# Packed means of one graph layer go to two tables, one for each half tile, and the node stage adds both

## What is computed

```python
h = jnp.maximum(_layernorm(x, axis=-1), 0.0)
msg = jnp.concatenate([h[src], edge_attr_128], axis=-1) @ W1 + b1
msg_sum = jax.ops.segment_sum(msg, dst, num_segments=N)
deg = jax.ops.segment_sum(jnp.ones((E,)), dst, num_segments=N)
node_msg = msg_sum / jnp.maximum(deg, 1.0)[:, None]
out = node_msg + (node_msg @ W2 + b2)
x = x + jnp.where(out >= 0, out, SLOPE * out)
```

## Time and profile before

| | before |
|---|---|
| median of three runs | 6092.15 us (6090.74 to 6095.57) |
| the profiled execution | 6094.43 us, of which the span is 6092.7 us |
| granted TensorE clock, mean | 0.813 |
| busy in the span | PE 62%, DVE 64%, POOL 49%, ACT 33% |
| stage e0 | first gather at 153 us, last store issued at 982 us |
| stage n0 | first load at 987 us, last scatter ends at 1534 us |

### The profile page before, as it was taken

One profiled execution on the slowest core, in us unless ns is written; L12 is line 12 of the kernel. 1 busy time (PEld: TensorE's weight loads), 2 busy tenths in 40 slices (PEclk: granted clock), 3 DMA queues, 4 the chain that ended last, 5 costly groups with the idle time before them and its releaser, 6 DMA issues. The chain is left out here.

```text
span 6092.7 us, 90449 instructions
## 1 busy us (share of the span) xinstructions
PE 3790.4 (62%) x17060; PEld 2576.8 (42%) x17060; DVE 3911.8 (64%) x12523; ACT 2020.2 (33%) x4450; POOL 2987.2 (49%) x2764
## 2 busy tenths in 40 slices
PE   0788884333079997669976557666600098888840
PEld 0466663333047776554445545555500043433310
DVE  8555555888058885334455546665568788888856
ACT  0444452333012222125556642222234433333310
POOL 0644442777177640000037767777710167777730
PEclk9888885555589999999986768988855599999975
DMA  6566665776955542774467767777678611111149
GB/s 224 148 158 159 159 158 155 232 220 201 352 146 136 143 116 59 235 242 155 152 201 234 229 197 143 132 131 130 108 226 272 196 34 38 43 46 48 48 151 377
DMA packets 983330, 994.95 MB, mean 163 GB/s; under 512 B 207537, under 2 KB 645313, under 8 KB 983059
## 3 DMA queue, kind: packets, MB, share of 16 engines
q1 hardware_dynamic: 673795, 628.11, 35.3%
q0 software_dynamic: 131904, 146.31, 12.5%
q10 hardware_dynamic: 177488, 218.95, 10.2%
HBM read 560.95 MB, written 466.16 MB: 169 GB/s over the span
## 5 line engine op out<-in xcount | busy, mean ns | idle before, releaser
L703 POOL DMA_INDIRECT at_first_table<-n_h,n_first_edge x784 | 791.2, 1009 | 1247.9 <-ACT n_h L271 890.6
L2467 PE MATMUL e_m<-e_by_rel,rel_w 128*128 128x512 f32 x1568 | 708.3, 606 | 0.0
L695 POOL DMA_INDIRECT e_xs<-x_table,e_idx x392 | 377.2, 962 | 515.4 <-POOLq L2357 396.2
L695 POOL DMA_INDIRECT e_x<-x,e_idx x392 | 375.1, 957 | 451.4 <-ACT e_h L271 232.8
L695 POOL DMA_INDIRECT e_hs<-h_table,e_idx x392 | 422.3, 1077 | 278.7 <-PE e_hs L1528 155.5
L2381 DVE SCALAR_TENSOR_TENSOR e_by_rel<-e_y,e_part_t 128x512 f32<-128x512 f32 x784 | 476.4, 679 | 28.1 <-PE e_y L2482 20.0
L703 POOL DMA_INDIRECT rel_sum_table<-e_res,e_again x392 | 393.8, 1005 | 148.9 <-issue 124.9
L2467 PEld LDWEIGHTS e_m<-e_by_rel,rel_w 128*128 128x128 f32 x1568 | 298.2, 195 | 340.3 <-issue 340.3
L2459 PE MATMUL e_t<-ident,e_part 128*128 128x128 f32 x392 | 67.1, 298 | 572.4 <-ACT e_part L271 440.0
L1008 PE MATMUL n_m<-n_mean,n_pick 128*128 128x129 f32 x784 | 203.4, 440 | 338.8 <-DVE n_pick L1073 315.2
L711 POOL DMA_INDIRECT sum_table<-e_res,e_target x196 | 309.7, 1580 | 133.2 <-issue 55.4
(11 more groups left out here) (372 smaller groups left out, 10391.2 us busy)
## 6 DMA issues: line engine op xcount, KB each, us to landing
x_table<-n_x ACTq DMA_DIRECT2D x294, 256.0 KB
n_x<-x_table SPq DMA_DIRECT2D x294, 256.0 KB
e_hd<-at_first_table SPq DMA_DIRECT2D x196, 256.0 KB
mean_runs_table<-e_packed SPq DMA_DIRECT2D x196, 130.0 KB
n_mean<-mean_runs_table SPq DMA_DIRECT2D x392, 65.0 KB
at_first_table<-prep_zero ACTq DMA_DIRECT2D x1, 25088.0 KB
e_edge<-edge128T SPq DMA_DIRECT2D x98, 256.0 KB
e_keep<-col_tab_table SPq DMA_DIRECT2D x196, 128.0 KB
```

Source lines behind the costliest of these rows:

```text
L695: pool.indirect_dma_start(out=tile[:, t, :], out_offset=None, in_=table, in_offset=bass.IndirectOffsetOnAxis(ap=idx[:, col + t:col + t + 1 ...
L703: pool.indirect_dma_start(out=table, out_offset=bass.IndirectOffsetOnAxis(ap=idx[:, t:t + 1], axis=0), in_=tile[:, t, :], in_offset=None, ...
L2467: ins = pe.matmul(flat(at(ps_m, u - 6)), k.rel_w[:, r, :], at(by_rel, u - 6)[:, r, :], start=(r == 0), stop=(r == RELS - 1))
```

## The change

`mean_runs` becomes two tables, `mean_runs[0]` for the halves 0 and `mean_runs[1]` for the halves 1. `e_packed` holds for each half four blocks, two with rows and two of zeros, and each store writes all four (512 rows of 520 bytes): since the other half's rows are now missing in a table, zeros must reach over their place. Each table has a chain of its own: `placed[h]` counts its landings, and a store waits only for the one before it in its own table. The stores keep their places in SP's body, each with a `sem_inc` more. ACT waits for the same two stores of step i - 15, now by two semaphores. At the start DVE zeroes the blocks behind the rows in all four buffers, and SP stores zeros over the first 256 rows of table 1. In n0 each of the four loads fetches 128 rows of both tables; the difference of destination and block is made for both (`near`), `k.local` is the greater of the two, `n_pick` is twice as wide, and PE adds the two by two matmuls into one sum, eight for each step.

```diff
@@ mean_edges
-        packed, packed_ready = ph.made("packed", [P, TILES, RUN_COLS], 4)
-        placed = ph.sem("placed")
+        packed, packed_ready = ph.made("packed", [P, HALVES, TILES, RUN_COLS], 4)
+        placed, packed_zero = [ph.sem(f"placed{h}") for h in range(HALVES)], ph.sem("packed_zero")
+        sp_turn = ph.sem("sp_turn")
@@ SP
-                if not (isinstance(j, int) and j == 0 and h == 0):
-                    sp.wait_ge(placed, (j * HALVES + h) * 16)
-                sp.dma_start(run_rows(scratch["mean_runs"], begins[2 * h], HALVES),
-                             at(packed, u)[:, HALVES * h:HALVES * h + HALVES, :]).then_inc(placed, 16)
+                if h or not (isinstance(j, int) and j == 0):
+                    sp.wait_ge(placed[h], (j + h) * 16)
+                sp.sem_inc(sp_turn, 1)
+                sp.dma_start(run_rows(scratch["mean_runs"][h], begins[2 * h], TILES), at(packed, u)[:, h, :, :]
+                             ).then_inc(placed[h], 16)
@@
                     sp.wait_ge(packed_ready, w + 1)
+                    sp.sem_inc(sp_turn, 1)
                     place_half(w, u, begins, 0)
@@
+            sp.wait_ge(packed_zero, 1)
+            sp.dma_start(scratch["mean_runs"][1, 0:HALVES * P, :].rearrange("(b p) d -> p b d", p=P),
+                         packed[0][:, 1, HALVES:TILES, :]).then_inc(placed[1], 16)
             run_steps(sp, body, S, 16, 20)
-            sp.wait_ge(placed, HALVES * 16 * S)
+            for h in range(HALVES):
+                sp.wait_ge(placed[h], 16 * (S + h))
@@ DVE
+            for slot in packed:
+                ins = dve.memset(slot[:, :, HALVES:TILES, :], 0.0)
+            ins.then_inc(packed_zero, 1)
@@ ACT
                     if begun(j - 4):
-                        act.wait_ge(placed, (j - 3) * HALVES * 16)
+                        for b in range(HALVES):
+                            act.wait_ge(placed[b], (j - 3 + b) * 16)
                     for b in range(HALVES):
-                        ins = act.activation(at(packed, u - 11)[:, HALVES * b:HALVES * b + HALVES, :], ps_c[b][:, :, :],
-                                             ACT.Copy)
+                        ins = act.activation(at(packed, u - 11)[:, b, 0:HALVES, :], ps_c[b][:, :, :], ACT.Copy)
@@ mean_nodes
-        mean, mean_in = ph.loaded("mean", [P, TILES, RUN_COLS])
-        local_ready = ph.sem("local_ready")
-        pick, pick_ready = ph.made("pick", [P, TILES, P])
+        mean, mean_in = ph.loaded("mean", [P, TILES, HALVES, RUN_COLS])
+        near, near_ready = ph.made("near", [P, TILES, HALVES])
+        pick, pick_ready = ph.made("pick", [P, TILES, HALVES, P])
@@ SP
-                        sp.dma_start(at(mean, u)[:, t, :], scratch["mean_runs"][bass.ds(begins[t], P), :]
+                        sp.dma_start(at(mean, u)[:, t, :, :],
+                                     scratch["mean_runs"][:, bass.ds(begins[t], P), :].rearrange("h p c -> p h c")
                                      ).then_inc(at(mean_in, u), 16)
@@ PE
-                        ins = pe.matmul(at(ps_m, u - 1)[t // HALVES][:, t % HALVES, :], at(pick, u - 1)[:, t, :],
-                                        at(mean, u - 1)[:, t, 0:D + 1], start=True, stop=True)
+                        for h in range(HALVES):
+                            ins = pe.matmul(at(ps_m, u - 1)[t // HALVES][:, t % HALVES, :], at(pick, u - 1)[:, t, h, :],
+                                            at(mean, u - 1)[:, t, h, 0:D + 1], start=(h == 0), stop=(h == HALVES - 1))
@@ DVE
-                    local = k.local[:, bass.ds(i, 1), :].rearrange("p a t -> p (a t)")
-                    dve.tensor_tensor(local, at(mean, u)[:, :, D + 1],
-                                      k.block_at[:, bass.ds(i, 1), :].rearrange("p a t -> p (a t)"), ALU.subtract
-                                      ).then_inc(local_ready, 1)
-                    dve.wait_ge(local_ready, i + 1)
+                    dve.tensor_tensor(at(near, u)[:, :, :], at(mean, u)[:, :, :, D + 1],
+                                      k.block_at[:, bass.ds(i, 1), :].rearrange("p a t -> p (a t)").unsqueeze(2)
+                                      .broadcast_to([P, TILES, HALVES]), ALU.subtract).then_inc(near_ready, 1)
+                    dve.wait_ge(near_ready, i + 1)
+                    dve.tensor_tensor(k.local[:, bass.ds(i, 1), :].rearrange("p a t -> p (a t)"), at(near, u)[:, :, 0],
+                                      at(near, u)[:, :, 1], ALU.max)
                     if begun(i - 2):
                         dve.wait_ge(mean_done, i - 1)
-                    dve.tensor_tensor(at(pick, u)[:, :, :],
-                                      k.place_row[:, 0:P].unsqueeze(1).broadcast_to([P, TILES, P]),
-                                      spread(local, P), ALU.is_equal).then_inc(pick_ready, 1)
+                    dve.tensor_tensor(at(pick, u)[:, :, :, :].rearrange("p t h c -> p (t h) c"),
+                                      k.place_row[:, 0:P].unsqueeze(1).broadcast_to([P, TILES * HALVES, P]),
+                                      spread(at(near, u)[:, :, :].rearrange("p t h -> p (t h)"), P), ALU.is_equal
+                                      ).then_inc(pick_ready, 1)
@@ kernel
-    scratch["mean_runs"] = table("mean_runs", (R + ROWS, RUN_COLS))
+    scratch["mean_runs"] = table("mean_runs", (HALVES, R + ROWS, RUN_COLS))
```

## The result

| | before | after |
|---|---|---|
| median | 6091.44 us (6087.42 to 6095.57) | 6222.77 us (6217.85 to 6226.75) |
| ratio, 95% interval | | 1.0215 (1.0197 to 1.0233) |
| the profiled execution, its span | 6094.43, 6092.7 us | 6217.85, 6216.1 us |
| granted TensorE clock, mean | 0.813 | 0.821 |

A forecast was written before the change was run, and what follows sets the result against it. A latency loop over ACT, PE and SP holding half 1's landing bounds e0, DVE bounds n0; +51 + 2.5 - 25 + 62 = +90 us gives 6182 us (72%), range 6140 to 6260 us.

The forecast's parts named there:

- The split chain in the steady part: Steady e0: half 0's store may issue earlier, but SP then waits longer at L773 for gates; no gain.
- Twice the bytes: Steady e0: each doubled store lands 0.55 us later, plus 0.05 us for sem_inc; +51 us over 85 steps.
- The start: Start of e0: four memsets and the store of zeros delay the first idx load; +2.5 us.
- The end: Last 12 steps of e0: the chain binds there, so two chains shorten them; -25 us, between -15 and -32.
- n0: Stage n0: DVE sets the pace; wider pick and added maximum cost 0.63 us a step, +62 us over 98 steps.
- The cover over PE: n0: PE's eight matmuls, 4.1 instead of 2.06 us, stay hidden behind DVE with some 1 us left.
- The chain sets the pace: Rival, e0: the chain of landings sets the step, so halving it gives -130 us in all, 5962 us; 8%.
- The DMA engines are crowded: Rival: e0's landing grows by 1.1 us and n0 loses its cover; +190 us, 6282 us; 11%.
- TensorE's clock: Rival, e0: PE runs more often at half speed, lengthening gates and transposes; +40 us, 6222 us; 6%.
- No change: Rival: gains at e0's end and in SP's 36 us of waits balance the costs; 3%.

The follow-up runs named there:

- e1b: Kernel before with only each store's bytes doubled (512 rows, half zeros; one table, one chain), n0 unchanged; 6173.76 us, ratio 1.0151.
- e5: Changed kernel with the maximum for k.local issued behind the pick instead of ahead of it; 6194.84 us, ratio 1.0185.
- e2: Kernel before with two tables and two chains, stores still 256 rows, table 0 zeroed in preparation, n0 reading table 0 only; 6777.25 us, one run.
- e3b: Kernel before with SP's load at L773 and its gate wait moved to the end of SP's body, repeated on another chip; 6021.75 us, ratio 0.9899.
- e4b: Changed kernel with SP's load and its gate wait moved to the end of SP's body, on the second chip; 6103.84 us, ratio 1.0033.
- c0: Control: the kernel before, unchanged, run on the third chip; 6789.46 us.
- e8: Kernel before with 384 rows in each store instead of 256, one table and one chain; 6817.4 us, single run.
- e9: Changed kernel with SP's gate-waiting load last and half 1's store directly behind half 0's; 6702.65 us, ratio 0.9894.
- e3: Kernel before with SP's load at L773 and its gate wait moved to the end of SP's body, first chip; 6691.51 us, ratio 0.9951.
- e4: Changed kernel with SP's load and its gate wait moved to the end of SP's body, first chip; 6679.44 us, ratio 0.9926.

## Why the prediction came out as it did

**The split chain in the steady part: nothing.** Right, and three runs bear on it: e1b without the split loses what the change loses, to 0.09 us a step (e5, same chip); e2 with the split alone shows no gain, though with no trace of before on its chip; and e3b gains 0.9 us a step by moving the one wait that the prediction named as the cover. The 5.81 us between the two issues and SP's waits at L773 were the right evidence; the large wait on ACT named the landing but not which of the two.

**Twice the bytes.** The term that was mis-sized. It was put at 0.55 us, near the floor of 0.43; the issue-to-copy piece grew by 0.78, in e1b by 0.75, and a store that runs alone by 0.6 to 0.7. The floor held for what it counted: 0.45 us more of packets in a store that runs alone. What was missing is that the time behind the last packet grows as well; in the loaded part the packet records give +0.30 us from first to last packet and +0.50 from there to the copy. Why is open. With 0.80 a step instead of 0.60 it is +68 instead of +51, inside the bounds. The Trainium skill's fit for a transfer ("DMA: Bandwidth & Descriptors", Anatomy of one DMA), which the page gives for transfers issued by GpSimd while SP issues these, gave 31 us; the measurement decides, and for these 520-byte rows it is more than double.

**The start.** +3.0 us at the first idx load (2.5 forecast) and +3.1 at the first copy. Another 1.4 us come between the first and the fifth copy, where the first stores run; which of them costs it I haven't traced.

**The end.** Right in kind, too large in size: -16, not -25. The stores of the last steps, against the earlier trace rows:

```profile
1010.51 26.82 SPq L755 DMA_DIRECT2D mean_runs_table<-e_packed  x15
...
1043.12 2.12 SPq L986 DMA_DIRECT2D n_mean<-mean_runs_table  x4
```

(26.82 - 0.41) / 14 = 1.89 us for a store, 3.8 for a step, where 3.1 was put. The step still waits for a landing, that of half 1 (12 waits, 8.8 us, from 1009 to 1046), and a doubled store takes 3.2 us when alone (e1b) and more with another beside it. The sum also left out what SP does by itself in a step: the 2.1 us between half 1's issue and the next half 0 that e2 shows stand here too.

**n0.** +0.74 us a step against +0.63. The pick was right (+0.53, 0.555 forecast). The maximum took 0.17 instead of 0.07: the nearest row had been two operations that write nothing for each other, while here each of three small operations has to start behind a wait or an address from a register; in the row the maximum starts 0.29 us behind the subtraction and the pick 0.08 us behind the maximum, and e5 gave 0.10 of it back. The 0.05 of `n_leaky` was not foreseen: it takes about 0.68 or 0.75 us, the longer in 1 of 98 steps before, 65 after, 36 in e4b and none in e5. So it goes with the maximum ahead of the pick; how is open. Together that would be +74 for 98 steps; the stage grew by 67, as POOL's scatters end closer behind DVE than before. The cover over PE held: 3.45 us of matmuls in the mean (the two rows have 3.81 and 3.64), not 4.1, since the clock rose (below). The DMA share was 0.82, forecast 0.81, and bound nothing.

**The rivals.** "The chain sets the pace" fell with e1b and SP's waits, and holds only once the wait for the gates is out of the way (e3b). "The DMA engines are crowded" was half right in e0, where the larger landing was its mechanism, and wrong in n0. "TensorE's clock" fell: in e0 0.86 is granted, as before (0.85), and the gates got no longer (1.41 and 1.36 us). That its 6222 us is what was measured is chance. "No change" fell: the gain at the end of e0 is 16 us, against 139 of costs.

All four terms missed to the same side, by 17, 9, 5 and 2 us; they make the 33 us between the 90 forecast and the 123 of the profiled executions, so nothing cancelled. The rest, 131 between the medians against 123, is spread of the runs.

## What to carry to other kernels

A wait says what came last, not which of several chains binds: follow one step round its loop and ask which landing has slack. A split of a chain that isn't in the loop gives nothing where the loop holds, and what it needs (here twice the bytes) is paid by the landing that is in it; a cheaper cure was to move one waiting load behind the stores, 1.0% with no work added. Cost a larger store by one that runs alone in the same trace and leave room for the time behind its last packet, and before splitting a chain look at the queue that both halves would share and at what its sequencer does between them.

## What the runs showed of the hardware

**A store's time behind its last packet grows with its bytes**, by 0.1 to 0.2 us alone and 0.50 us under load for 256 rows more of 520 bytes. In the steady part of e0 it is, up to ACT's copy, 0.66 us for 256 rows (c0 0.65), 0.86 for 384 (e8), 1.06 to 1.15 for 512 (e1b, after) and 2.3 when two stores of 512 run one behind the other (e9). The Trainium skill ("DMA: Bandwidth & Descriptors", Queues, rings and completion order) has a transfer's signal land only after all earlier writes of its DMA engine; that would let the time grow with the writes under way. The runs agree in direction, e9 most of all, but none of them separates this from another cause.

**TensorE's clock in n0 rose from 0.50 to 0.69** from 1200 to 1300 us, with PE busy 39% before and 54% after, and to 0.62 from 1100 to 1500 us. Before, it is at the lower of its two levels (1.2 GHz) all through; after, it spends some 40% of the first stretch and 24% of the second at 2.4 GHz. The prediction worked out 4.1 us of matmuls from lengths at half speed, and they took 3.45 us in the mean. The Trainium skill ("TensorE: Matmul & The Clock Gate", The HAM clock gate) has it in this direction, that activity releases the clock.

**The same kernel takes 6082, 6725 and 6777 us on three chips.** Single operations are as long as before, but engines idle more, in stages that no edit touches too. The picks of the control, in 480 us of n0, against the earlier trace rows:

```profile
1020.00:1500.00 480.00, 47.03 (x68) 0.50 0.57 168
```

47.03 us for 68 picks and 62.23 for 90 are both 0.69 us each, but there are fewer of them. The added idle time is uneven over the four bodies of a loop turn (steps of n0 in c0 take 5.4, 5.9, 7.9 and 8.7 us in turn, before 5.0, 5.2, 5.0 and 5.9), so it lies around the turns of the hardware loops; its cause is open. It matters for the experiments: on such a chip moving the load gained 0.5% in the kernel before (e3) and 0.7% against it in the changed one (e4, intervals that overlap), while on the chip of e3b and e4b the first gains 1.0% and the second loses 0.3%. The verdicts on the loop rest on the latter, which behaves as the traces of before and after do.
